# Cross attention of 16 heads: the turn of the row maxima moved between the second row phase and the weighing, and into the first bank of scores

## The reference, cut to what matters

```
q = layernorm(x) @ Wq          # (8, 100, 16 heads, 16)
k, v = ctx @ Wk, ctx @ Wv      # (8, 361, 16 heads, 16)
scores = q @ k.T / 4           # per sequence and head: 100 x 361
attn = softmax(scores)         # the row's maximum is subtracted in the exponent
x = x + (attn @ v) @ Wo
```

## Time and profile before

| what | us |
|---|---|
| three runs | 1505.01, 1495.36, 1498.7 |
| median | 1498.7 |
| the profiled execution: its own time | 1495.78 |
| its span, first to last instruction | 1494.0 |
| mean granted TensorE clock in it (share of full speed) | 0.954 |

### The profile page before, as it was taken

One profiled execution on the slowest core, in us unless ns is written; L12 is line 12 of the kernel. 1 busy time (PEld: TensorE's weight loads), 2 busy tenths in 40 slices (PEclk: granted clock), 3 DMA queues, 4 the chain that ended last, 5 costly groups with the idle time before them and its releaser, 6 DMA issues. The chain is left out here.

```text
span 1494.0 us, 31527 instructions
## 1 busy us (share of the span) xinstructions
PE 1353.9 (91%) x12488; PEld 1054.5 (71%) x12488; DVE 769.4 (52%) x1733; ACT 646.7 (43%) x1683; POOL 194.9 (13%) x200
## 2 busy tenths in 40 slices
PE   7999899989989899899999889989957896899887
PEld 6776668866557588778999765669955675578632
DVE  3666677655556677520000477501127485566765
ACT  3444226633366366344444246432225674256300
POOL 3000250000024200050110420040042000300000
PEclk9999999989999999899999989989988997999999
DMA  6000331011301200366996100545211000700100
GB/s 217 1 1 1 68 65 22 4 44 43 80 8 21 46 11 4 130 210 244 343 342 261 49 22 1 227 166 202 74 52 40 1 2 1 118 5 4 68 1 22
DMA packets 43943, 120.19 MB, mean 80 GB/s; under 512 B 11931, under 2 KB 28440, under 8 KB 38412
## 3 DMA queue, kind: packets, MB, share of 16 engines
q1 hardware_dynamic: 33048, 62.04, 14.4%
q0 software_dynamic: 7616, 53.12, 10.3%
q10 hardware_dynamic: 3136, 3.03, 0.7%
HBM read 95.78 MB, written 11.00 MB: 71 GB/s over the span
## 5 line engine op out<-in xcount | busy, mean ns | idle before, releaser
L826 PE MATMUL wide<-early_kt,early_q 32*100 32x361 f32 x512 | 95.4, 485 | 2.8 <-PEq L66 1.6
L2555 ACT ACTIVATE l1f_hidden<-wide,l1f_pack 128x128 f32<-128x128 f32 x160 | 58.8, 368 | 78.0 <-PE wide L2494 68.1
L2677 DVE TENSOR_TENSOR l1f_out<-summed,l1f_pack 128x256 f32<-128x256 f32 x20 | 8.5, 425 | 152.8 <-PE summed L2502 152.8
L2494 PEld LDWEIGHTS wide<-l1f_rt,l1f_pack 128*128 128x128 f32 x640 | 74.5, 192 | 1.7 <-issue 0.8
L2494 PE MATMUL wide<-l1f_rt,l1f_pack 128*128 128x128 f32 x640 | 74.8, 275 | 0.6 <-ACT l1f_rt L2545 0.6
L113 PE MATMUL summed<-ident 128*128 128x128 f32 x302 | 44.4, 314 | 33.2 <-PEq L66 33.2
L2502 PE MATMUL summed<-l1f_pack,l1f_hidden 128*128 128x256 f32 x320 | 72.4, 379 | 0.0
L113 PEld LDWEIGHTS summed<-ident 128*128 128x128 f32 x302 | 42.2, 226 | 38.9 <-issue 38.9
L2502 PEld LDWEIGHTS summed<-l1f_pack,l1f_hidden 128*128 128x128 f32 x320 | 59.2, 190 | 7.2
L3688 PE MATMUL wide<-l3f_we,l3f_xt 128*100 128x512 f32 x128 | 59.6, 620 | 1.2 <-DVE l3f_acc L3756 1.2
L1220 DVE TENSOR_REDUCE l3x_mx<-wide 100x2 f32<-100x722 f32 x64 | 55.3, 904 | 3.2 <-PE wide L826 3.0
(11 more groups left out here) (605 smaller groups left out, 3369.8 us busy)
## 6 DMA issues: line engine op xcount, KB each, us to landing
l2f_w<-l2f_w_dram SPq DMA_DIRECT2D x16, 1024.0 KB, 11.5
ctxt<-ctxt_dram SPq DMA_DIRECT2D x4, 1083.0 KB, 17.1
early_kt<-soon_kd SPq DMA_DIRECT2D x32, 90.8 KB, 3.3
l1f_sorted_x<-l1f_zeros SPq DMA_DIRECT2D x4, 640.0 KB
l1f_rows<-l1f_sorted_x SPq DMA_DIRECT2D x20, 128.0 KB, 7.5
l1f_sorted_y<-l1f_out ACTq DMA_DIRECT2D x20, 128.0 KB, 9.4
l0f_w<-l0f_w_dram SPq DMA_DIRECT2D x18, 128.0 KB, 2.1
l1f_shared<-l1f_shared_dram SPq DMA_DIRECT2D x1, 2180.0 KB, 9.0
```

The source lines that it names most:

```text
L826: pe.matmul(wide[0:S, i, 0:SKV], q4[R * i:R * (i + 1), g % 2, b, g // 2, :], kt[R * i:R * (i + 1), g % 2, b, g // 2, 0:SKV], start=True, s ...
L2494: last = pe.matmul(wide[:, f % 4, 0:P], w1_of(w, k, f), rt[:, n % 2, k, :], start=k == 0, stop=k == KC - 1)
L2555: act.activation(hidden[:, f, 0:P], wide[:, f % 4, 0:P], ACT.Gelu, bias=b1_of(pack[:, n % SLOTS, :], f)).then_inc(sem["h_ready"], 1)
L2677: dve.tensor_tensor(out[:, n % 2], summed[:, n % 2, 0:E], b2_of(pack[:, n % SLOTS, :]), ALU.add).then_inc(sem["y_ready"], 1)
```

## The change

Four edits belong together.

- On the PE `turn_maxima(n)` moves from the head of the turn to the place between the second row phase and `weigh(n-2)`.
- It writes to bank 0 of `wide` in place of bank 2. It now waits for `m_ready` 2n + 3 (the reduction of pair 0 of quad n + 1, which reads bank 0), and for `q2_ready` n (the addition of the quad before has read bank 0).
- On DVE the wait of `with_maxima` for the scores of quad n + 1 goes, and it reads bank 0.
- The order on DVE becomes `highest(n+1, 1)`, `with_maxima(n)`, `highest(n+2, 0)`.

```
 def turn_maxima(n):
-    pe.wait_ge(sem["m_ready"], 2 * n + 2)
-    pe.transpose(wide[:, 2, LOW:LOW + S], mx[:, n % 2, :], net.ident[0:S, 0:S]).then_inc(sem["mt_psum"], 1)
+    pe.wait_ge(sem["m_ready"], min(2 * n + 3, 2 * QUADS))
+    if n >= 1:
+        pe.wait_ge(sem["q2_ready"], n)
+    pe.transpose(wide[:, 0, LOW:LOW + S], mx[:, n % 2, :], net.ident[0:S, 0:S]).then_inc(sem["mt_psum"], 1)
...
 for n in range(QUADS + 2):
-    if n < QUADS:
-        turn_maxima(n)
     if n + 1 < QUADS:
         score(n + 1, 1)
...
         score_by_key(n - 1, (2, 3))
+    if n < QUADS:
+        turn_maxima(n)
     if n >= 2:
         weigh(n - 2)
...
 def with_maxima(n):
     dve.wait_ge(sem["mt_psum"], n + 1)
-    if n + 1 < QUADS:
-        dve.wait_ge(sem["s_psum"], Q * (n + 2))
...
-    dve.tensor_tensor(q2[:, n % 2, :], q4[:, g % 2, b, g // 2, :], wide[:, 2, LOW:LOW + S], ALU.add).then_inc(sem["q2_ready"], 1)
+    dve.tensor_tensor(q2[:, n % 2, :], q4[:, g % 2, b, g // 2, :], wide[:, 0, LOW:LOW + S], ALU.add).then_inc(sem["q2_ready"], 1)
...
-for n in range(1, QUADS + 1):
-    if n < QUADS:
-        highest(n, 0)
-    with_maxima(n - 1)
-    if n < QUADS:
-        highest(n, 1)
+highest(1, 0)
+for n in range(QUADS):
+    if n + 1 < QUADS:
+        highest(n + 1, 1)
+    with_maxima(n)
+    if n + 2 < QUADS:
+        highest(n + 2, 0)
```

## The result

Median of 22 runs of the changed kernel: 1508.87 us (1503.64 to 1525.03). The kernel before, 22 runs: 1499.54 us (1494.71 to 1508.12). The ratio is 1.0068, 95% interval 1.0048 to 1.0088: slower by 10.2 us, 7.2 to 13.2, by the ratio (the medians differ by 9.3). The forecast was 1512 in a range of 1502 to 1522, a cost of 14.5. The profiled execution of after took 1505.21 us with a span of 1503.4.

What follows compares the result with a forecast made beforehand. DVE's dependencies and PE's work, level near 2.38 us a turn, were taken as the bound; the ACT ring at 2.55 would replace them. Adding 4.99, 4.81, 4.26 and 0.48 gave 14.5 us, so 1512, range 1502 to 1522.

Steps and rivals of the forecast that it cites:

- 11.8 us that DVE waited: DVE idle before its addition, 24 times in 60 us; removing that wait would not bring the idle back as time.
- ACT ring: Weighing, take, head 3's exponential, scores by key (2, 3), next weighing: 2.31 us, growing by the transpose's 0.24 to 2.55.
- PE's own sum: PE's phases and changes of tile shape in one turn: 2.39 us, less at most a few hundredths after the change.
- One sign: PE weight loads idle some 0.1 to 0.2 us at scores by key (2, 3) in the changed kernel.
- second wait: An added wait on the moved transpose: put at 0, at most 0.05 us if it costs a step.
- A: Rival, chance 0.12: transpose to weighing 0.29 plus 0.05 for another wait, 2.65 a turn, 1519 to 1522 us.
- B: Rival, chance 0.12: scores by key do not wait for head 3's exponential; 2.35 to 2.39 a turn, 1493 to 1499 us.
- C: Rival, chance 0.06: DVE's dependencies alone set the turn, which falls from 2.38 to 2.33; 1491 to 1494 us.
- new DVE ring: Transpose, addition, reduction of pair 0, second phase, transpose: 2.33 us a turn, hardly below the earlier 2.36.
- start of the loop: First turns without a weighing, 2.36 before and 2.33 after, transpose one phase later: together 0, give or take 0.2 us.
- three disturbed turns of `l3x`: Turns 1305.63 to 1318.93, holding a 3.66 us stall and what follows: each lengthens by 0.16, together 0.48 us.
- Everything outside the loops is unchanged: Rest of the kernel got no term; a stall elsewhere could shift the time without touching the argument.

Runs made afterwards that it cites:

- e1: Changed kernel, head 3's exponential reading head 2's scores and standing ahead of the take: 1493.55 us, ratio 0.9973 to the kernel before.
- e10: Kernel before with a second, long-met wait (`q2_ready`) on the transpose at its old place: 1497.7 us, ratio 0.9987 to the kernel before.
- e2: Kernel before, head 3's exponential reading head 2's scores and standing ahead of the take: 1499.71 us, ratio 0.9998 to the kernel before.
- e8: Changed kernel profiled once more without any edit: 1522.3 us.
- e4: Kernel before profiled once more without any edit: 1503.91 us.
- e9: Kernel before with a pause of 40 small, drained VectorE instructions behind `l1x`: 1503.07 us, ratio 1.0028 to the kernel before.
- e3: Changed kernel with the transpose at its new place but writing the old bank 2, with the waits that needs: 1537.24 us in one run.
- e6: Changed kernel with an extra transpose between the moved transpose and the weighing: 1523.69 us in one run.
- e7: Kernel before with an extra transpose ahead of the turn of the maxima: 1504.06 us in one run.

## Why the prediction was right, point by point

**The mechanism held in its main steps.** The 11.8 us that DVE waited were no time to be won: most of that wait went, and the time did not come back. The ACT ring of 2.31 took in the transpose at 0.24 and became 2.55, and each link has the forecast length: 0.12 behind the exponential, 0.84, 0.23 to 0.24, and 0.34 from the transpose to the addition (262.45 to 262.79). The turns lie at 2.546, inside the 2.54 to 2.56 named. The PE's own sum is 2.40 in e1, where the ACT ring is open, against "2.39, less at most a few hundredths". One sign did not appear: PE weight loads were to lie idle for 0.1 to 0.2 ahead of scores by key (2, 3), and other loads fill that time. The second wait cost nothing, as taken: scores by key to transpose is the same 0.84 in after as scores by key to weighing was the earlier trace rows, and e10 agrees at the old place. The Trainium skill's "TensorEngine Tiling (Array Packing)", section Tiling Modes, has a change of mode drain the TensorE. The 0.10 between the end of the transpose's load and the weighing's first (264.99 + 0.14 to 265.23) is in line with that; no run here tells a drain from another cause of the gap.

**The rivals.** A (2.65 a turn) is out by the 2.546. B is out by the 0.11 to 0.12 behind head 3's exponential in every turn, and by e1 and e2 together. C is out by the turn of e1: with the ACT ring open, the next limit, PE at 2.40, lies 0.07 over the new DVE ring of 2.33. The Trainium skill's "Perfetto Trace Analysis", section Identifying the Most-Contended Engine, judges PE by the share of its weight loads; that share is 63.74 of 74.10, 86%, in `l1x` of after, and 59.46 of 69.50, 86%, in `l0x` of e1. Here that share does not tell the two apart: it is the same in a kernel bound by a ring and in one bound by PE.

**The start of the loop** was put at 0, give or take 0.2: from the first reduction to the first weighing it took 10.20, 8.63 and 8.70 before and 10.30, 8.81 and 8.88 after, 0.1 to 0.2 more a call.

**What was mis-sized is the sum, 14.5 us, against 10.2 (7.2 to 13.2) measured.** The loops did their part. With the medians of after, against the values of the forecast: 29 x (2.546 - 2.378) + 29 x (2.547 - 2.384) + 29 x (2.546 - 2.386) = 14.2. With stalls it depends on the execution: from the first to the thirtieth weighing the three calls took 224.3 in after and 230.3 in e8, 213.4 in before and 210.0 in e4. Two assumptions failed. The first moves the profiled execution, the second is the term that the sum lacked; the range held because it was wide enough for both.

- *The three disturbed turns of `l3x` keep their stall.* I took them over with 0.16 each. Their size was chance, and the profiled after had smaller ones, one of 1.08 for instance:

```profile
1317.74 0.28 PEld L842 LDWEIGHTS summed<-l3x_q,late_kt 32*121 32x121 f32 x3
1319.10 0.60 PEld L842 LDWEIGHTS summed<-l3x_q,late_kt 32*121 32x121 f32 x9 [1.08 <-issue]
```

  That is why `l3x` as a stage looks unchanged between the two profiled executions, 123.40 and 123.49, while its undisturbed turns are 0.16 longer. It shifts the profiled time; what such stalls do to the medians is not shown.

- *Everything outside the loops is unchanged.* I wrote only that a stall elsewhere could shift the time, and gave it no term. It is about -4 us, the 10.2 less the 14.2 of the loops (-7 to -1 by the interval), and the runs with their mean clock suggest where it comes from: of before beside e1 and e9, the eight runs at 0.955 took 1494.22 to 1498.16, mean 1496.56; the four runs of after at 0.955 took 1505.9 to 1511.58, mean 1508.84. At equal mean clock the difference is 12.3. But the runs of before lie lower, at medians of 0.951 and 0.953 in two sets of 19, against 0.9555 in after; straight lines through these three sets of runs give 1.1 to 1.5 us for each 0.001, so that is 3 to 7 us. The loops' 14 us at full clock lift the mean clock by less than 0.001 themselves. And e1, whose loops are not longer, lies at 0.955 too, and is faster than before by 4.1 us (0.3 to 7.8, from its ratio) though its turns are 0.01 to 0.04 longer.

The stage in which the traces show this is the layer-3 self attention: 148.5 to 154.8 with the transpose at the old place, mean 152.2 of five, and 147.3 to 147.7 at the new one, six of six. That is 4.6 us, the size of what is missing, but from three long traces of five against none of six, of kernels that differ among themselves. The whole span less the 29 turns of each call says the same less sharply: 1280.5 to 1292.1 in those five, mean 1287.9, and 1279.2 to 1290.2 at the new place, mean 1282.7 of five (e3, whose loops also start later, left out). The two profiles of after alone lie at 1279.2 and 1290.2. So the sum lacked a term for the clock outside the loops; that the change itself moves that clock is suggested by this and not shown. Why a trace has the long stretch at half clock or not is open. Arrival time was tried with e9, without a verdict.

Where that stage is alike, turns and time agree: after and e1 have the transpose at the same place and the same self attention, and differ by 1508.87 - 1493.55 = 15.3 in the medians and by 224.3 - 209.0 = 15.3 in the turns of their traces. That the two come out equal is partly luck: 87 x (2.546 - 2.398) = 12.9 of the turns is the ring, the rest is mostly stalls, and the two medians are from different sets of runs.

**No better version came out of it.** e1 shows what an open ring is worth at the new place, but it leaves out the scores of head 3. To keep them they need a bank that the weighing does not write, and all eight banks of `wide`, `turned` and `summed` are in use in the loop.

## What to carry to other kernels

Ask of a moved instruction not only which wait it removes, but which ring of dependencies it enters; an engine that waits once a turn for another has a ring that can be added up from three or four rows, and the stretches at a loop's start and end, where little else is queued, show its links bare. A delay of 0.23 us on PE cost 0.01 a turn outside such a ring, one of 0.16 cost 0.16 inside it, and busy shares did not tell the two apart. If you put in an instruction to price it, look whether its own wait holds it, as it did in e6. And a sum over turns of loops is not yet a sum for the run: give what lies outside, above all the clock there, a spread of its own, from several runs.

## What the runs showed of the hardware

- Two transposes on PE in a row load 0.06 apart where nothing is waited for (e7, 261.69 to 261.75, and the few turns of e6 in which ACT was early). At a change of the tile's shape in this loop 0.10 lies idle behind a transpose's load and 0.15 behind a weighing's last one.
- From the end of DVE's reduction to the transpose that waits for it 0.05 passes, and the same from the end of ACT's exponential to the extra transpose of e6. To the scores by key in after it is 0.11 to 0.12. They wait for two semaphores, and the trace of after has an instruction of 0.05 on PE's queue for the second wait (L839, 186 times). That would explain the difference, and an exchange of the two waits might take 0.05 out of the ring; no run tried it.
- Runs of one kernel spread by 16 us with their mean clock: of the 38 of before beside e1 and e9 the one at 0.944 took 1508.79, those at 0.955 took 1494.22 to 1498.16.
